# TensorE sums raw image rows for two streams of the first quad ahead of their normalisation; part sums by halves; another order on ScalarE; the last product in two halves

## What is computed

```python
def _L0_conv_ref(x, weight, bias):    # 9x9 Gaussian kernels built from (sx, sy, angle) per (out, in) channel, zero padding 4
    ...
def _L1_conv_ref(x, weight):          # 5x5 convolution, reflected edges (written with FFTs)
    ...
x = x + _L0_conv_ref(_gn(x), L0_conv_weight, L0_conv_bias)   # _gn: group norm, 16 groups, eps 1e-5
x = x + _L1_conv_ref(_gn(x), L1_conv_weight)
```

## Time and profile before

| | us |
|---|---|
| median of 3 runs | 245.91 (245.87 to 245.93) |
| the profiled execution | 245.87 |
| its span, first to last instruction | 244.0 |
| TensorE busy | 224.7 (92%) |
| VectorE busy | 214.8 (88%) |
| ScalarE busy | 153.9 (63%) |

### The profile page before, as it was taken

The page is one execution under the profiler, slowest core; times in us unless marked ns, Lnnn a source line. Parts: engine busy times, 40 slices in busy tenths (PEclk is TensorE's granted clock), DMA queues, the critical chain, the costliest instruction groups (busy, mean ns, idle before and its releaser), DMA issues.

```text
span 244.0 us, 4070 instructions
## 1 busy us (share of the span) xinstructions
PE 224.7 (92%) x1402; PEld 139.2 (57%) x1402; DVE 214.8 (88%) x463; ACT 153.9 (63%) x325; POOL 4.4 (2%) x12
## 2 busy tenths in 40 slices
PE   0076999999999999999999999999999999999994
PEld 0074556666666666555666665556666665655552
DVE  5989999999999999999989998999997459978942
ACT  5798698799399557999537592537358003569210
POOL 1000000050000000000000000000000000000000
PEclk9999799999999999999999999999999999999999
DMA  6970222320016000003422000063020002522023
GB/s 166 414 323 1 66 67 63 76 70 8 0 31 177 6 3 1 0 3 99 132 80 97 0 0 3 17 169 126 1 97 3 0 0 60 148 101 83 18 97 97
DMA packets 9188, 17.69 MB, mean 73 GB/s; under 512 B 3408, under 2 KB 6096, under 8 KB 9168
## 3 DMA queue, kind: packets, MB, share of 16 engines
q1 hardware_dynamic: 8352, 17.16, 21.8%
q10 hardware_dynamic: 816, 0.28, 0.4%
HBM read 5.51 MB, written 4.72 MB: 42 GB/s over the span
## 4 chain that ended last, share of the span: by engine, by line
PE 85%; DVE 6%; ACT 3%; DMA 2%; issue 1%; SPq 1%
PE banks L1329 52%; PE banks L1346 33%; ACT P L1032 2%; DMA whl<-work 2%; DMA prm<-in_w 1%; DVE arg L480 1%; SPq L376 1%; DVE s L466 1%; DVE whl L534 1%; DVE sums L475 1%; ACT L1128 1%; ACT junk L1014 0%; PE banks L1297 0%; DVE lo L696 0%; DVE work L525 0%
## 5 line engine op out<-in xcount | busy, mean ns | idle before, releaser
L1329 PE MATMUL banks<-hi,whl 128*128 128x360 f16 (+4 forms) x576 | 99.9, 323 | 2.9 <-ACT hi L1055 2.4
L1329 PEld LDWEIGHTS banks<-hi,whl 128*128 128x128 f16 x576 | 56.6, 99 | 37.6 <-ACT whl L1082 2.5
L1329 PE MATMUL banks<-lo,whl 128*128 128x376 f16 (+4 forms) x288 | 52.0, 321 | 0.0
L1014 ACT ACTIVATE junk<-X 128x576 bf16<-128x576 f32 x58 | 39.5, 681 | 2.7 <-DMA X<-in_x 0.5
L1329 PEld LDWEIGHTS banks<-lo,whl 128*128 128x128 f16 x288 | 28.1, 98 | 17.3 <-DVE lo L696 0.2
L1346 PE MATMUL banks<-hi,wl 128*128 128x384 f16 x160 | 31.6, 328 | 0.0
L1346 PE MATMUL banks<-lo,wh 128*128 128x384 f16 x160 | 31.6, 328 | 0.0
L1346 PE MATMUL banks<-hi,wh 128*128 128x384 f16 x160 | 31.6, 328 | 0.0
L1055 ACT CAST hi<-work 128x416 f16<-128x416 f32 x32 | 16.6, 538 | 19.9 <-PE banks L1346 14.1
L1055 ACT CAST hi<-s 128x384 f16<-128x384 f32 x32 | 15.3, 508 | 19.3 <-DVE s L663 11.7
L1045 ACT ACTIVATE work<-work,gof,gsc 128x26 f32<-128x26 f32 (+1 forms) x48 | 23.3, 576 | 3.6 <-DVE gof L614 3.6
(11 more groups left out here) (125 smaller groups left out, 223.6 us busy)
## 6 DMA issues: line engine op xcount, KB each, us to landing
X<-in_x SPq DMA_DIRECT2D x8, 576.0 KB, 9.4
out<-X SPq DMA_DIRECT2D x7, 576.0 KB, 2.8
work<-X SPq DMA_DIRECT2D x8, 432.0 KB, 3.8
whl<-work SPq DMA_DIRECT2D x32, 64.0 KB, 2.0
work<-X SPq DMA_DIRECT2D x8, 144.0 KB, 3.6
stage<-in_w SPq DMA_DIRECT2D x1, 640.0 KB, 7.3
work<-X SPq DMA_DIRECT2D x32, 12.0 KB, 2.3
out<-X SPq DMA_DIRECT2D x1, 384.0 KB, 2.6
```

What stands on the lines that cost most here:

```text
L1014: nc.scalar.activation(waste, image(n, m), function, accum_out=sums[c][:, col:col + 1]).then_inc(sums_done[c], 1)
L1329: ins = nc.tensor.matmul(dst[:, :, o0:o1], w[1][:, i, t * P:(t + 1) * P], src[:, :, o0 + dx:o1 + dx], start=(first and part == 0 and t == ...
```

## The change

- **Streams 1 and 2 of the first quad on TensorE.** Twelve fp32 matmuls of 128 x 384 (`near_rows`) add raw rows of `X`, each times the identity or a multiple of it (`factors1`, three 128 x 128 matrices made by ScalarE), into PSUM banks 4 and 5. Two run ahead of `stats(1, 0)`, ten behind it. ScalarE scales and offsets stream 1 out of PSUM (`first_stream1`, 4 instructions of 128 x 96), VectorE scales stream 2 (`first_stream2`, 2 of 128 x 192). `first_near_sum` (4 instructions) and `stream1(0, 1)`, `stream1(0, 2)` go. VectorE computes one more small vector, `off1`. `WARMING` is 4, and TensorE no longer waits for the exponentials ahead of it. The table of constants has 128 more columns (the identity).
- **A and B in halves.** `near1(0)` and `far1(0)` (128 x 768) become four `first_half` of 128 x 384: two before streams 0 and 7, two before the wide streams. The first waits for all four normalised images.
- **ScalarE's order.** The normalisation of the first quad is spread between casts and copies; the channel sums of the next quad's first three images and the Sqrt table load come later. `rest_of_turn` lets ScalarE issue two of the four DMAs of the mirrored kernels of streams 1 and 2. SyncE sends the fp16 high part of kernel 1 as soon as it is copied and its low part later; TensorE waits for the low part (`turned_low`) only at the third fp16 part.
- **The last product in halves**, in banks 2 and 3, with two evictions (`last_end2`) and two stores.

```diff
-WARMING = 20
+WARMING = 4
...
+NEAR_FACTORS = (-4.25, -1.0, 4.25)
+NEAR_OFFSET = 2.0 * (1.0 + 1.0 - 4.25)
+NEAR_BANK = {1: 4, 2: 5}
...
             def turn(at, i):
 
+
+                if at == 0:
+                    sp.wait_ge(turning, 1)
+                    for k in range(RB):
+                        sp.dma_start(turned_to(i, k)[:, 0:1, :], turned_from(at, k)[:, 0:1, :]).then_inc(turned[MIRROR[i]], 16)
                 sp.wait_ge(turning, 2 * (at + 1))
-                for k in range(RB):
-                    sp.dma_start(whl[(RB - 1 - k) * C:(RB - k) * C, :, MIRROR[i], NT * P:],
-                                 turn_at[k * C:(k + 1) * C, at % TURNS, :, :]).then_inc(turned[MIRROR[i]], 16)
+                for k in range(RB if at > 1 else RB // 2):
+                    if at == 0:
+                        sp.dma_start(turned_to(i, k)[:, 1:2, :], turned_from(at, k)[:, 1:2, :]).then_inc(turned_low, 16)
+                    else:
+                        sp.dma_start(turned_to(i, k), turned_from(at, k)).then_inc(turned[MIRROR[i]], 16)
...
+                stt(off1[:, :], mean, -NEAR_OFFSET, gsc[1][:, :], ALU.mult, ALU.mult).then_inc(small[1], 1)
...
-            def first_near_sum(h):
-
-                at = slice(h * TILES1, (h + 1) * TILES1)
-                dve.wait_ge(norm_done[1], IMG * (h + 1))
-                part(tt(part_two("U")[:, at, :], d1_two(1)[:, at, :], d1_two(5)[:, at, :], ALU.add))
-                dve.wait_ge(parts_done, 2 * h + 1)
-                part(stt(part_two("U")[:, at, :], d1_two(3)[:, at, :], -4.25, part_two("U")[:, at, :], ALU.mult, ALU.add))
+            def first_stream2():
+
+                dve.wait_ge(near_mm, 2)
+                dve.wait_ge(s_done[1], 1)
+                for h in range(2):
+                    at = slice(h * TILES1, (h + 1) * TILES1)
+                    by_image = gsc[1][:, h * IMG:(h + 1) * IMG].unsqueeze(1).unsqueeze(3).to_broadcast([P, TILES1, IMG, W])
+                    ins = tt(by_image1(s32_1[:, 2, :])[:, at, :, :], by_image1(banks[:, NEAR_BANK[2], 0:OUTN])[:, at, :, :], by_image, ALU.mult)
+                ins.then_inc(s_done[1], 1)
+
+            def first_half(key, which, one, other):
+
+                dve.wait_ge(norm_done[1], QI)
+                part(tt(which(key), d1(one), d1(other), ALU.subtract))
...
+            def last_end2():
+
+                n, k = NP - 1, 3
+                dve.wait_ge(out_done[2], 5 * n + 3)
+                for h, bank in enumerate((BANKS2[n][k], LAST_BANK)):
+                    at = slice(h * TILES2 // 2, (h + 1) * TILES2 // 2)
+                    dve.wait_ge(conv_mm[2], 4 * n + k + 1 + h)
+                    src = banks[:, bank, 0:HALF2].rearrange("p (t y) -> p t y", y=ROW)
+                    stt(out2(n, M2 - 1)[:, at, :], src, osc2[:, k:k + 1], out2(n, M2 - 1)[:, at, :], ALU.mult,
+                        ALU.add).then_inc(out_done[2], 1)
...
                 done(stt(flat1, flat1, W_SCALE, krec[:, :].unsqueeze(1).to_broadcast([P, NT * RB, C]), ALU.mult, ALU.mult))
                 MARK["weights", 1] = count[0]
                 kernel_scale()
-                for h in range(2):
-                    first_near_sum(h)
-                stream1(0, 1)
+                low_half(1, 0, 0)
+                first_stream2()
+                scaled(block1(1), "block1")
                 low_kernel(1)
-                low_half(1, 0, 0)
-                stream1(0, 2)
-                scaled(block1(1), "block1")
                 made_two()
                 low_half(1, 0, 1)
-                near1(0)
                 low_kernel(2)
+                scaled(block1(0), ("weights", 0))
+                first_half("A", even, 2, 4)
                 end_part1(0, 0)
                 stream1(0, 0)
-                scaled(block1(0), ("weights", 0))
-                far1(0)
+                first_half("B", odd, 5, 3)
                 low_half(1, 0, 2)
                 low_kernel(0)
                 end_part1(0, 7)
@@ -825,6 +873,8 @@
                 low_kernel(7)
                 dve.wait_ge(dve_w, MARK["base4"])
                 made(3, block1(1), 2.0, slot(4), ALU.mult, ALU.add)
+                first_half("A", odd, 1, 3)
+                first_half("B", even, 6, 4)
                 first_wide1(0)
                 stream1(0, 3)
                 dve.wait_ge(dve_w, MARK["weights", 3])
...
+                act.wait_ge(near_mm, 1)
+                act.wait_ge(small[1], SMALL)
+                for i in range(QI):
+                    h, m = i // IMG, i % IMG
+                    at = slice(h * TILES1, (h + 1) * TILES1)
+                    ins = nc.scalar.activation(by_image1(s32_1[:, 1, :])[:, at, m, :], by_image1(banks[:, NEAR_BANK[1], 0:OUTN])[:, at, m, :],
+                                               ACT.Identity, bias=off1[:, i:i + 1], scale=gsc[1][:, i:i + 1])
+                ins.then_inc(s_done[1], 1)
...
+            def rest_of_turn(i):
+
+                at = FIRST_ORDER.index(i)
+                act.wait_ge(turning, 2 * (at + 1))
+                for k in range(RB // 2, RB):
+                    if at == 0:
+                        act.dma_start(turned_to(i, k)[:, 1:2, :], turned_from(at, k)[:, 1:2, :]).then_inc(turned_low, 16)
+                    else:
+                        act.dma_start(turned_to(i, k), turned_from(at, k)).then_inc(turned[MIRROR[i]], 16)
...
             nc.scalar.activation(sc[:, :, :], frac[:, :, :], ACT.Sin, scale=TWO_PI).then_inc(sin_done, 1)
             act.wait_ge(consts_set, 1)
             nc.scalar.activation(warm[:, :], bias_c[2][:, :], ACT.Exp)
+            near_factors((0,))
             channel_sums(1, 0)
+            near_factors((1, 2))
             kernel_exponentials()
-            channel_sums(1, 1, range(1))
-            normalise1(0)
-
-            nc.scalar.activation(warm[:, :], bias_c[2][:, :], ACT.Sqrt)
+            first_stream1()
+            high_half(1, 0, 0)
+            normalise1(0, range(2))
             high_kernel(1)
-            high_half(1, 0, 0)
             turn_kernel(1, wh)
+            high_half(1, 0, 1)
+            normalise1(0, range(2, 3))
+            high_kernel_two()
             turn_kernel(1, wl)
-            high_half(1, 0, 1)
-            high_kernel_two()
+            rest_of_turn(1)
+            normalise1(0, range(3, 4))
             turn_kernel(2, wh)
+            high_kernel(0)
             turn_kernel(2, wl)
+            rest_of_turn(2)
             high_half(1, 0, 2)
-            high_kernel(0)
-            channel_sums(1, 1, range(1, 2))
             turn_kernel(0, wh)
             turn_kernel(0, wl)
-            channel_sums(1, 1, range(2, 3))
             high_half(1, 0, 3)
             high_kernel(7)
+            channel_sums(1, 1, range(1))
             turn_kernel(7, wh)
             turn_kernel(7, wl)
+            channel_sums(1, 1, range(1, 2))
             act.wait_ge(bias_loaded, 16)
             high_kernel(3)
             high_half(1, 0, 4)
             turn_kernel(3, wh)
+            channel_sums(1, 1, range(2, 3))
             high_kernel(4)
             turn_kernel(3, wl)
             high_half(1, 0, 5)
@@ -1160,6 +1239,8 @@
             turn_kernel(5, wh)
             high_kernel(6)
             turn_kernel(5, wl)
+
+            nc.scalar.activation(warm[:, :], bias_c[2][:, :], ACT.Sqrt)
             high_half(1, 0, 7)
             standard_deviation(1, 1)
...
-            act.wait_ge(out_done[2], 5 * NP)
-            act.dma_start(tile_rows(dram_pair(out, NP - 1))[:, :, 2 * ROW:], tile_rows(pair(NP - 1))[:, :, 2 * ROW:]).then_inc(stored, 16)
+            for h in range(2):
+                at = slice(h * TILES2 // 2, (h + 1) * TILES2 // 2)
+                act.wait_ge(out_done[2], 5 * NP + h)
+                act.dma_start(tile_rows(dram_pair(out, NP - 1))[:, at, 2 * ROW:],
+                              tile_rows(pair(NP - 1))[:, at, 2 * ROW:]).then_inc(stored, 16)
...
+            def near_rows(i, steps):
+
...
+                dst = tiled1(banks[:, NEAR_BANK[i], 0:OUTN])
+                for step in steps:
+                    if i == 1 and step == 4:
+                        pe.wait_ge(factors_made, 1)
+                    if i == 2 and step == 2:
+                        pe.wait_ge(factors_made, len(NEAR_FACTORS))
+                    row, factor = terms[step]
+                    ins = nc.tensor.matmul(dst, factor, out1(0, row), start=(step == 0), stop=(step == len(terms) - 1))
+                if steps[-1] == len(terms) - 1:
+                    ins.then_inc(near_mm, 1)
...
+                    if qd == 0 and not first and part == 2 and i == 1:
+                        pe.wait_ge(turned_low, 16 * RB)
...
+                rows = TILES2 * IMG
+                if (n, k) == (NP - 1, 3):
+                    conv2(n, k, bank, slice(0, rows // 2))
+                    pe.wait_ge(*held[LAST_BANK])
+                    conv2(n, k, LAST_BANK, slice(rows // 2, rows))
+                else:
```

(16 more changed lines are left out.)

52 lines of the change are left out of this document (34 added, 18 removed).

## The result

| | us |
|---|---|
| changed kernel, median of 8 runs | 248.23 (247.11 to 249.27) |
| before, median of 8 runs beside them | 245.92 (245.87 to 246.22) |
| ratio | 1.0089, 95% interval 1.0073 to 1.0106 |
| profiled execution of the changed kernel | 247.24, its span 245.5 |

Slower by 0.9%, so the direction is that of the forecast; the median lies 0.3 above the range. The single times show more than the median. Before, eight runs lie within 0.35 us. Two questions follow: why 247.2 instead of 246.8, and where the spread comes from.

A forecast was written before the change was run, and what follows sets the result against it. It took VectorE and ScalarE to set TensorE's pace up to 79.98 us. 245.87 + 1.1 (middle) - 0.25 (end) = 246.7, 247.0 with the later start; it said 246.8 us, range 244.5 to 247.9.

The forecast's parts named there:

- the reading of who holds whom: Up to the layer 2 statistics at 79.98 us, VectorE and ScalarE already set TensorE's pace, with no slack.
- The rival of 241.2: Start-up: TensorE's earlier start carries through, 2.7 + 1.5 + 0.5 us, giving 241.2; partly surviving, 244.5; chance 0.08.
- the rival that they are cheap: ScalarE's four DMA issues cost less than 0.64 us each: 246.1 to 246.4, chance 0.13; nearly free, 244.4, chance 0.12.
- the middle: VectorE's account up to the first quad's last low half (49.67 us before): +1.1 us, +1.35 with ScalarE's later start.
- (a): VectorE's work up to the last low half: sums and streams out, smaller items in, -2.35 us.
- (b): VectorE's added waits there: 1.5 images, 1.4 third cast, 1.0 sixth cast, 0.5 standard deviation, 0.1 a kernel: 4.5 us.
- (c): Ahead of VectorE's stretch, which began at 18.7 us: 0.1 us more, for `off1`.
- The small gaps: Part of VectorE's 1.68 us idle in the stretch, behind its own semaphores: they stay; the other 1.0 counts as waits for ScalarE.
- the end: Last product, evictions and store in halves: -0.25 us, at worst +0.2.
- Raw sums late: Rival at the start-up: clock level low until 16.8 us, products at 1.2 us, stream 1 at 16.1: +1.2, 248.0; chance 0.08.
- the level rising on the way as it did in the warm-up: Raw sums on TensorE: the clock rises during them, so ScalarE starts stream 1 at 14.5 to 15.2 us.
- What was foreseen of the clock: After TensorE's 2.6 us wait before kernel 0's product, 1.2 GHz may return, costing 1.5 us, with 2.5 us to spare.

The follow-up runs named there:

- the late run: The changed kernel run again with no edit, to see the raw sums in a slow run: 249.28 us.
- both edits: Changed kernel with all four mirror DMAs of kernels 1 and 2 issued by SyncE and 11 fp32 warm-up matmuls ahead of the raw sums: 243.92 us, ratio 0.9922.
- GpSimd's image: On top of both edits, the fourth image of the first quad normalised by GpSimd instead of ScalarE: 244.35 us, ratio 0.9939.
- The doses: Two runs, each on top of both edits: 5 more fp32 matmuls on TensorE before kernel 0's first product, 243.96 us; one more `low_kernel(0)` on VectorE, 244.67 us.
- warmed ahead: Changed kernel with eleven fp32 matmuls of 128 x 128 on TensorE ahead of the raw sums: 247.25 us, ratio 1.0050.
- one pair: Changed kernel with the 11 warm-up matmuls, kernel 1's two issues kept on ScalarE, kernel 2's two moved to SyncE: 245.61 us, ratio 0.9986.
- SyncE's issues: Changed kernel with all four DMAs of the mirrored kernels 1 and 2 issued by SyncE, none by ScalarE: 243.94 us, ratio 0.9926.

## Why the prediction was right and where it was wrong

**Right: the reading of who holds whom.** "A delay of theirs in the first quad arrives at 79.98 in full, a gain of TensorE alone does not." In all fourteen traces the last low half and the statistics move together, 30.3 us apart: 49.67 and 79.98 before, 51.64 and 81.97 after, 53.70 and 84.01 in the late run, 48.29 and 78.60 with both edits, 48.88 and 79.20 with GpSimd's image. The doses agree: VectorE +0.75 for 0.73, TensorE nothing for 0.8. The rival of 241.2 (TensorE's early start carries through) is out: TensorE stood at kernel 0's product with 3.11 us to wait (forecast 2.6).

**Right: the cause.** The forecast put the loss on four issues in ScalarE's queue with ScalarE idle, against the rival that they are cheap. Removing them is worth 3.3 us (247.25 to 243.92, both warmed ahead), one pair about half of it. The Trainium skill ("DMA: Bandwidth & Descriptors", Issuing engines are not separate DMA queues) calls the sequencer time that issuing on several engines saves usually small; here an issue held ScalarE for 0.63 to 0.87 us, and as every one of them lay on the chain, the price was four issues and the gaps.

**Mis-sized, the middle: +1.1 forecast, +1.97 measured.** (The forecast's terms add up to 1.15.) By the terms of VectorE's account: (a) Work, -2.35 with 0.1 for `off1`, so -2.45 behind the first kernel; measured there -2.30: 0.15. (b) Waits 4.5: measured 1.75 for the images (1.5), 1.73 for the third cast (1.4), 0.99 for the sixth (1.0), 0.57 for the standard deviation (0.5), sum 5.04: 0.5. Of (b) the first two carry the excess, and the chain shows it: the pairs took 1.42 and 1.58 us instead of 1.28, since ScalarE's issues were 0.63, 0.76, 0.68 and 0.87, where SyncE's median of the same DMA is 0.6, and with the gaps around them ScalarE stood 1.56 and 1.65. (c) What stands ahead of the stretch: put at 0.1, `off1` alone, measured 0.32. The other 0.2 is a term that the forecast had at nothing: VectorE's first instruction starts at 3.05 instead of 2.79. The small gaps, taken as unchanged, went from 0.7 to 0.6.

**Mis-sized, the end: -0.25 forecast, -0.5 measured.** The half matmuls at 84 ns were as forecast, with their weight loads hidden. The store of 96 KB landed in 1.8, where the 2.0 of a 64 KB DMA of another kind had been taken, and 192 KB had taken 2.1.

Together 245.87 + 2.0 - 0.5 = 247.4 against 247.24; the rest, 0.1, lies outside the span. That is inside the forecast's own range, 246.3 to 247.4, helped by luck: the two errors have opposite signs.

**Wrong: a chance, and with it the number.** "Raw sums late", given 0.08, is what more than half of the runs showed, by their times in part or whole: five of eight are above 247.9. Its mechanism was described as it happens (products at the lower level, ScalarE late by them); its size was short, since the products began at 11.76 instead of 11.3 and took 1.28 to 1.35 us each instead of 1.2, so that ScalarE started at 17.27 instead of 16.1: 2.04 instead of 1.2. The range was also drawn too narrow for this rival as it stood: its own 248.0 lies above the upper end, 247.9. The step that failed is "the level rising on the way as it did in the warm-up". The one trace of before showed one moment of rising, and I took it for a property of the program. In the kernel before, the late rise could hide: TensorE's warm-up was no one's input until 22 us, so the eight nearly equal times of before said nothing on it. The change put the first input of ScalarE's chain behind matmuls that run at whatever level there is.

The Trainium skill ("TensorE: Matmul & The Clock Gate", What's actually happening) says that the number of matmuls at the lower level differs from run to run of one kernel; it puts the loss by that level at a kernel's start under 1% of a typical span and advises against fitting a certain number. The traces agree with the first: the raw sums behind `stats` at the lower level are none in the run of 247.24 and four in that of 249.28. The prediction should have weighed it. The difference between the two runs, 2.04 of 247 us or 0.8%, is within that size, but it is as much as the whole verdict here.

**What was foreseen of the clock and didn't matter.** A stretch at the lower level after the wait of kernel 0 came in the run warmed ahead and not in the run of 247.24; in neither was the end affected, since VectorE held it.

**What stays open.** Why the level rises by 11.5 us in one run and after 17 in another, with the same instructions at the same times, no run here tells. That it decides the spread is shown by the traces and by its absence after the early warm-up. One run of five of the kernel with both edits took 0.7 more than the other four, and one of five with GpSimd's image 0.5 more; no trace shows them. Why ScalarE's issues are longer than SyncE's is open too: in each trace that has them, SyncE issues at the same moments.

## What to carry to other kernels

An engine that issues a DMA is held by it, here for 0.4 to 0.9 us, by the kind of transfer; before moving issues from one queue to another, look whether the receiving engine stands on the chain. Here 3.3 us of 247 lay in four instructions, and undoing them turned a loss of 0.5% into a gain of 0.8%. When work on TensorE becomes the first input of a chain, its cold price counts, and a kernel that never showed a spread can get one: take several runs, and put matmuls that nobody waits for ahead of it (here eleven took the spread from 2 us to 0.05). A wait that is removed by reordering one engine shows up at the next instruction behind the work that was pushed back: sum the engine's work between its deadlines before moving it.

## What the runs showed of the hardware that was not expected

- The moment at which TensorE reaches its higher level after a cold start differs from run to run: the same raw sums cost 0.65 to 0.69 us each from 11.5 us on in one execution, 1.28 to 1.35 up to 17 us in another, and with SyncE's issues the rise stands between, near 13. The granted clock of the windows reads 1.00 in both, so only the durations show it; the factor of two is that of the levels 1.2 and 2.4 GHz.

```profile
11.00:18.00 7.00, 6.72 (x14) 3.96 (x14) 6.31 (x24) 3.17 (x8) 0.00 (x0) 1.00 0.84 344
```

```profile
11.00:18.00 7.00, 6.75 (x23) 4.14 (x23) 6.31 (x24) 5.25 (x11) 0.00 (x0) 1.00 0.85 348
```

  (First the run of 249.28, with 14 records, then that of 247.24, with 23, in the same 7 us.) The Trainium skill ("FP8 and Floating Point Precision", TensorE Precision Notes) has true fp32 as 4 passes; an estimate from it, 4 x 384 cycles at the two levels, is 1.28 or 0.64 us for 384 columns, and the traces agree at both (1.28 to 1.35, 0.65 to 0.69).
- The same kind of DMA takes longer to issue from ScalarE's queue than from SyncE's: 0.63 to 0.87 against 0.51 to 0.67 in the same run, the second of each pair by 0.13 to 0.19 more than the first. Both queues issued at once there; neither alone was measured for ScalarE.
- Two fp32 instructions of VectorE with two inputs took longer beside GpSimd: 0.82 became 1.13 and 0.42 became 0.73. A third, which had begun 0.26 us before GpSimd's first (14.68 and 14.94), took its usual 0.82. GpSimd's own instructions were shorter there (2.21 us for two) than at 50 us in the kernel before (3.5 for two).
